# Six transposed rows instead of eight in block 1, two pair sums on GpSimd, and new call orders

## The chip, the cores and the metric

One core of one Trainium2 chip. The metric is the device time of one execution in microseconds. The kernel before takes 512.92 us, the median of three runs (512.43 to 513.56). TensorE multiplies matrices (PE in the profile; its weight loads are PEld), VectorE is DVE, ScalarE is ACT, GpSimd is POOL, and SyncE (SP) only issues DMAs.

## The reference

The input is 8 sequences of 1024 tokens with 128 features. Per token and head (16 heads of 8 columns) a state of 8 by 8 is decayed and added to, and read with the query; then come a layer norm, a gate, an output projection, a residual with its layer norm, and a feed-forward net of ternary weights with a second residual and norm.

```python
def step(state, inp):
    qt, kt, vt, gt = inp
    state = state * gt[..., None] + vt[..., None] * kt[..., None, :]
    out_t = jnp.einsum('bhij,bhj->bhi', state, qt)
    return (state, out_t)
...
out = (out - mu) * rsqrt(var + EPS) * gamma + beta
out = (out * silu(x @ Wg)) @ Wout
x = layernorm(x + out)
h = silu(tlin(x, w1_w, w1_s)) * tlin(x, w2_w, w2_s)
h = gelu(tlin(h, h1_w, h1_s))
h = gelu(tlin(h, h2_w, h2_s))
x = layernorm(x + tlin(h, w3_w, w3_s))
```

## The kernel before

**Blocks.** The 8192 tokens are cut into 16 blocks of 512; two blocks make a sequence. All products are float32. For each block n the attention half makes five projections of the transposed input (K, Q, F, V, gate; L2234), sends K and Q out to DRAM and fetches them back spread over the partitions as eight rows j of 512 tokens (KJ and QJ, 128 x 4096 each). VectorE and GpSimd multiply K by V (`kv`, `kv_gp`), VectorE runs one scan per row (`scan(n, j)`, L1582) and multiplies Q by the state, two rows at a time (`qs(n, p)`, L1589, p = 0 to 3).

**The sum of the eight rows.** For blocks 2 to 15, VectorE adds pairs down to one (`add(n, p)`, L1597, three calls), GpSimd adds the last two rows (`add_gp(n)`, L550), and TensorE transposes that single row, one 128 x 128 transpose for each of four chunks (`sum_transposed(n)`, L2293). Block 1 (`EARLY`, L27) leaves the adding to TensorE: for each chunk it transposes eight rows into the same PSUM accumulation, 32 transposes, and waits for all four `qs`. Block 0 has its own code (`kvj`, `qsj`, `sum_j`).

**Behind the sum.** `stats_o` (DVE), `rstd_of(n, "o")` (POOL), `norm_o` (ACT), `transpose_y` (PE), `affine` (ACT), `gated_y` (POOL), `attention_out` (PE), `residual_1` and `stats_1` (DVE), `rstd_of(n, "1")` (POOL), `norm_1` (ACT), `transpose_x1` (PE), `x1_hi` (ACT), `x1_lo` (DVE). Then the feed-forward half of the block: `up_hi`/`up_lo`, `mid_open`/`mid_hi`/`mid_lo` for two layers (all L2325) and `last_begin`/`last_rest` (L2424). Every activation is split into a high part on ACT (`hi`, L899) and a low part on POOL (`lo`, L482).

**What sets the order.** Each engine runs one list of calls, written out by hand in the file, from L562 (POOL), L989 (ACT), L1718 (DVE), L308 on (SP, the DMA queue) and L2465 on (PE). An engine works through its list strictly in order, and each call waits for semaphores. The attention half of block n+1 is interleaved with the feed-forward half of block n on all engines. The same queue order holds for DMAs: all transfers but one are issued by SP.

**The start.** Before the feed-forward lists, PE runs the attention of block 0 and part of block 1, with filler products that nobody reads (`keep_busy`, L2230; `keep_busy(16, F[3])` at L3171 is 16 of them). ACT copies the feed-forward weights to another format in four pieces (`split_weights(k)`, L967, L969) and sums the low halves of their bits (`sum_low_parts(k)`, L971, L980). DVE and PE make of these sums a flag (`find_low_parts`, `count_low_parts`, `set_flag`, L1716). PE waits for the flag behind `project_q(2)`, loads it (L3179) and branches to `rest(False)` or `rest(True)`: the feed-forward products, `up_hi(0, 0)` first, stand behind that branch. `center_w3` (L938, with L943 and L947) removes the mean of the last weight matrix on ACT, after `scale_w3` on POOL (L558); `last_begin(0)` needs it. `tanh(3)` (L828) reads the same PSUM bank that `project_gate(2)` writes next.

Of the kernel before, what the change touches and what calls it, by code (L numbers as in the profile page):

```python
# [3 lines left out]
def build_program(nc, x_d, xT_d, wproj_d, wffn_d, w3_d, w3s_d, cols_d, ident_d, out_d):  # L4
# [10 lines left out]
    P, T, HD = 128, 512, 8  # L15
# [11 lines left out]
    EARLY = range(1, 2)  # L27
    XB, XTB, GB = 4, 4, 3
# [9 lines left out]
    with ctx:  # L38
# [84 lines left out]
        def adds_gpsimd(n):  # L123
            return sum(m not in EARLY for m in range(1, n))

# [119 lines left out]
        def _(e):  # L245
            def load_x(n):
# [8 lines left out]
                4: (qj_made, 8), 5: (gate_made, 2), 6: (q_made, 2), 7: (v_made, 4), 8: (gate_made, 5), 9: (v_made, 6), 10: (gate_made, 7), 11: (gate_made, 8), 12: (gate_made, 9), 13: (gate_made, 10), 14: (gate_made, 11), 15: (v_made, 12),  # L255
# [73 lines left out]
            send(1, 1)  # L329
            load_weights(2)  # L330
            fetch(1, 1, 0)
            fetch(1, 1, 1)
# [3 lines left out]
            load_x(0)  # L336
            send(2, 1)
            load_xT(4)
            fetch(1, 0, 0)
            fetch(1, 0, 1)  # L340
            fetch(2, 1, 0)
            send(3, 1)
            send(2, 0)
            fetch(2, 1, 1)
            fetch(2, 0, 0)
            send(3, 0)
            load_x(1)
            fetch(2, 0, 1)
            fetch(3, 1, 0)
            fetch(3, 1, 1)  # L350
            load_x(2)
            send(4, 1)
            send(4, 0)
            load_xT(5)
            fetch(3, 0, 0)
            fetch(3, 0, 1)
            fetch(4, 1, 0)
            fetch(4, 1, 1)
            load_x(3)
            fetch(4, 0, 0)  # L360
            send(5, 0)
            load_x(4)
            send(5, 1)
            store(0)
            fetch(4, 0, 1)
            fetch(5, 1, 0)
            load_xT(6)
            load_x(5)
            fetch(5, 0, 0)
            load_xT(7)  # L370
            fetch(5, 0, 1)
            fetch(5, 1, 1)
            send(6, 1)
            fetch(6, 1, 0)
            load_x(6)
            send(6, 0)
            store(1)
            load_x(7)
            fetch(6, 1, 1)
            store(2)  # L380
            fetch(6, 0, 0)
            fetch(6, 0, 1)
            send(7, 1)
            fetch(7, 1, 0)
            load_xT(8)
            load_x(8)
            fetch(7, 1, 1)
            load_xT(9)
            send(7, 0)
            load_x(9)  # L390
            send(8, 1)
            fetch(7, 0, 0)
            fetch(7, 0, 1)
            fetch(8, 1, 0)
            send(8, 0)
            store(3)
            load_xT(10)
            send(9, 1)
            fetch(8, 0, 0)
            fetch(8, 1, 1)  # L400
            load_x(10)
            fetch(8, 0, 1)
            load_xT(11)
            store(4)
            load_xT(12)
            send(9, 0)
            fetch(9, 1, 0)
            fetch(9, 1, 1)
            fetch(9, 0, 0)
            fetch(9, 0, 1)  # L410
            send(10, 1)
            send(10, 0)
            fetch(10, 1, 0)
            fetch(10, 0, 0)
            send(11, 1)
            fetch(10, 1, 1)
            store(5)
            fetch(11, 1, 0)
            store(6)
            load_x(11)  # L420
            fetch(11, 1, 1)
            load_x(12)
            send(11, 0)
            load_xT(13)
            fetch(10, 0, 1)
            fetch(11, 0, 0)
            fetch(11, 0, 1)
            store(7)
            send(12, 1)
            send(12, 0)  # L430
            fetch(12, 1, 0)
            fetch(12, 1, 1)
            fetch(12, 0, 0)
            send(13, 0)
            send(13, 1)
            fetch(12, 0, 1)
            load_xT(14)
            fetch(13, 1, 0)
            fetch(13, 0, 0)
            store(8)  # L440
            fetch(13, 1, 1)
            load_x(13)
            send(14, 1)
            fetch(13, 0, 1)
            load_x(14)
            load_xT(15)
# [3 lines left out]
            load_x(15)  # L450
            store(9)
            fetch(14, 0, 0)
            fetch(14, 0, 1)
            send(15, 1)
            fetch(15, 1, 0)
            fetch(15, 1, 1)
            store(10)
# [18 lines left out]
        def _(e):  # L476
# [87 lines left out]
            scale_w3()  # L564
            qsj_gp(1)
            kvj_gp(2)
            kvj_gp(4)
            qsj_gp(2)
# [3 lines left out]
            kv_gp(1, 5)  # L572
            rstd_of(0, "o")
            kv_gp(1, 6)
# [5 lines left out]
            rstd_of(1, "o")  # L580
            kv_gp(2, 6)
            lo(1, 0, 3)
# [10 lines left out]
            rstd_of(2, "o")  # L593
            lo(1, 1, 2)
            lo(1, 1, 3)
            kv_gp(3, 6)
# [3 lines left out]
            kv_gp(3, 7)  # L600
            lo(2, 1, 1)
            rstd_of(2, "1")
            lo(2, 1, 2)
            lo(2, 1, 3)
            add_gp(3)
            lo(1, 2, 0)
            kv_gp(4, 6)
            rstd_of(3, "o")
            lo(1, 2, 1)
            lo(1, 2, 2)  # L610
            lo(1, 2, 3)
            kv_gp(4, 7)
# [3 lines left out]
            lo(2, 2, 2)  # L616
            rstd_of(3, "1")
            lo(2, 2, 3)
            add_gp(4)
            rstd_2(1)  # L620
            lo(1, 3, 0)
            lo(1, 3, 1)
            lo(1, 3, 2)
            rstd_of(4, "o")
            lo(1, 3, 3)
            rstd_2(2)
            kv_gp(5, 6)
# [2597 lines left out]
```

## Time and profile before

| | us |
|---|---|
| median of three runs | 512.92 |
| the profiled execution | 513.06 |
| its span | 511.3 |
| PE busy | 500.1 |
| DVE busy | 448.2 |
| ACT busy | 404.9 |
| POOL busy | 310.0 |

The profile lists the busy time of each engine and, for groups of instructions, how many there are, how long one takes and what ended the idle time before them. A busy PE is not a PE at its peak: its matmuls are pipelined, a record covers the time from issue to the last result, and the records of neighbours overlap, so that the pace is read from the start of one group to the start of the next. A product of 512 float32 columns appears as two records. The timeline gives the start of each group in microseconds from the start of the span, its length, and the idle time before it with the instruction that ended it.

### The profile page before, as it was taken

The numbers are of one execution on the slowest core, as the hardware profiler recorded it, in microseconds if no ns is written. First come the engines' busy times: TensorE is split into PE (matmuls) and PEld (weight loads), VectorE is DVE, ScalarE is ACT, GpSimd is POOL, SyncE is SP. The second block draws the span as 40 slices with busy tenths as digits, with TensorE's granted clock in tenths as the row PEclk, the third lists the DMA queues.
The fourth block names the chain that finished last, engine by engine and source line by source line (L and its number), as shares of the span: only waits on it lengthen the run. The fifth ranks groups of instructions, "written<-read, shape, count | busy, mean of one in ns | idle before, by whom it ended". The sixth has DMA issues, their size and how long they took to land.

```text
span 511.3 us, 7950 instructions
## 1 busy us (share of the span) xinstructions
PE 500.1 (98%) x2524; PEld 382.4 (75%) x2524; DVE 448.2 (88%) x707; ACT 404.9 (79%) x837; POOL 310.0 (61%) x363
## 2 busy tenths in 40 slices
PE   8999999999999999999999999999999999999995
PEld 4566777777878777787877877787777777787895
DVE  4799899999999999999999899999999999992352
ACT  4766778788897888889798887988787897878863
POOL 1651856848393856848385774828477674929431
PEclk9999999999999999999999999999999999999999
DMA  6988999809978666987988992389858870700001
GB/s 203 254 251 201 248 235 272 210 2 251 243 167 225 144 153 174 219 220 203 237 201 187 252 251 68 110 200 214 197 137 213 204 182 7 185 22 1 22 2 65
DMA packets 21500, 87.33 MB, mean 171 GB/s; under 512 B 2512, under 2 KB 3280, under 8 KB 13520
## 3 DMA queue, kind: packets, MB, share of 16 engines
q1 hardware_dynamic: 21312, 86.53, 68.1%
q8 instruction: 22, 0.36, 0.3%
q10 hardware_dynamic: 144, 0.26, 0.1%
q14 instruction: 22, 0.18, 0.1%
HBM read 74.72 MB, written 12.06 MB: 170 GB/s over the span
## 4 chain that ended last, share of the span: by engine, by line
PE 74%; POOL 10%; issue 8%; ACT 4%; DVE 3%; POOLq 0%; DVEq 0%; ACTq 0%
PE F L2325 43%; PE front L2234 8%; PE back L2424 8%; PE ps_v L2234 3%; POOL h2lo L482 3%; POOL h1lo L482 2%; PE back L2218 2%; PE back L2311 2%; PE back L2234 1%; PE F L2230 1%; ACT h L906 1%; PE back L2293 1%; POOL KJ L544 1%; DVE h L1646 1%; POOL QJ L550 1%
## 5 line engine op out<-in xcount | busy, mean ns | idle before, releaser
L482 POOL TENSOR_TENSOR h1lo<-h,h1hi 128x512 fp32r<-128x512 f32 x60 | 76.4, 1289 | 21.3 <-ACT h1hi L899 21.0
L906 ACT ACTIVATE h<-F,cols 128x512 f32<-128x512 f32 x120 | 79.9, 687 | 9.1 <-PE F L2325 8.1
L550 POOL TENSOR_TENSOR QJ<-QJ 128x512 f32<-128x512 f32 x14 | 17.9, 1281 | 110.3 <-DVE QJ L1597 110.3
L482 POOL TENSOR_TENSOR h2lo<-h,h2hi 128x512 fp32r<-128x512 f32 x60 | 76.3, 1291 | 5.0 <-ACT h2hi L899 4.5
L1582 DVE TENSOR_TENSOR_SCAN KJ<-g,carry,KJ 128x512 f32<-128x512 f32 x64 | 78.1, 1263 | 0.4 <-ACT carry L832 0.2
L2325 PE MATMUL F<-h2hi,whi 128*128 128x512 f32 (+1 forms) x256 | 76.7, 429 | 0.7 <-ACT h L906 0.4
L1582 DVE TENSOR_TENSOR_SCAN KJ<-g,KJ 128x512 f32<-128x512 f32 x64 | 74.3, 1203 | 2.6 <-POOL KJ L531 2.4
L2325 PE MATMUL F<-h1hi,whi 128*128 128x512 f32 (+1 forms) x256 | 71.4, 417 | 1.1 <-DVE h L1646 0.7
L1589 DVE TENSOR_TENSOR QJ<-QJ,KJ 128x1024 f32<-128x1024 f32 x60 | 71.5, 1218 | 0.2
L2325 PE MATMUL F<-h2lo,whi 128*128 128x512 f32 (+1 forms) x256 | 65.9, 399 | 0.0
L2325 PE MATMUL F<-h1lo,whi 128*128 128x512 f32 (+1 forms) x256 | 65.3, 397 | 0.0
L2234 PE MATMUL front<-xT,wproj 128*128 128x512 f32 x122 | 63.3, 601 | 0.8 <-ACT qk L822 0.6
L2325 PEld LDWEIGHTS F<-h2hi,whi 128*128 128x128 f32 x256 | 46.9, 189 | 22.2 <-issue 8.4
L2325 PEld LDWEIGHTS F<-h1hi,whi 128*128 128x128 f32 x256 | 45.6, 188 | 22.7 <-issue 9.5
L2424 PEld LDWEIGHTS back<-w,h 128*128 128x128 f32 x480 | 57.6, 192 | 2.6 <-DVE x1lo L1641 0.7
L2424 PE MATMUL back<-w,h 128*128 128x128 f32 x480 | 58.4, 275 | 0.0
L893 ACT ACTIVATE h<-F,cols 128x512 f32<-128x512 f32 x60 | 40.5, 686 | 17.5 <-PE F L2325 17.2
L2325 PEld LDWEIGHTS F<-h2lo,whi 128*128 128x128 f32 x256 | 45.7, 189 | 11.7 <-POOL h2lo L482 2.1
L2325 PEld LDWEIGHTS F<-h1lo,whi 128*128 128x128 f32 x256 | 46.2, 188 | 11.1 <-issue 1.4
L1566 DVE TENSOR_TENSOR KJ<-ps_v,KJ 128x1024 f32<-128x1024 f32 x44 | 52.7, 1209 | 1.4 <-ACT v_sb L867 1.4
L1597 DVE TENSOR_TENSOR QJ<-QJ 128x1024 f32<-128x1024 f32 x42 | 51.2, 1219 | 1.4
L1646 DVE SCALAR_TENSOR_TENSOR h<-F,cols,h 128x512 f32<-128x512 f32 x60 | 44.0, 744 | 6.1 <-ACT h L893 5.7
(176 smaller groups left out, 930.0 us busy)
## 6 DMA issues: line engine op xcount, KB each, us to landing
KJ<-qk_bounce SPq DMA_DIRECT2D x30, 1024.0 KB, 11.8
QJ<-qk_bounce SPq DMA_DIRECT2D x30, 1024.0 KB, 12.4
qk_bounce<-qk SPq DMA_DIRECT2D x30, 256.0 KB, 3.4
x_in<-in_x SPq DMA_DIRECT2D x16, 256.0 KB, 8.5
xT<-in_xT SPq DMA_DIRECT2D x15, 256.0 KB, 9.8
out<-res SPq DMA_DIRECT2D x15, 256.0 KB, 3.8
wraw<-in_wffn SPq DMA_DIRECT2D x2, 1024.0 KB, 10.3
wraw<-in_wffn SPq DMA_DIRECT2D x2, 256.0 KB, 4.5
```

Of the source, the lines that this page charges most:

```text
L482: e.tensor_tensor(h_lo[layer][:, t, :w], h[:, t, :w], h_hi[layer][:, t, :w].bitcast(f32), ALU.subtract).then_inc(lo_done[layer], 1)
L550: e.tensor_tensor(first, first, other, ALU.add).then_inc(add_gp_done, 1)
L893: e.activation(h[:, t, :WIDTH[n]], F[2 * (t % 2)][:, :WIDTH[n]], ACT.Silu, scale=S1[t]).then_inc(silu_done, 1)
L906: e.activation(dst[:, t, :WIDTH[n]], F[t][:, :WIDTH[n]], ACT.Gelu, scale=scale[t]).then_inc(gelu_done[layer], 1)
L1566: e.tensor_tensor(K, vb, K, ALU.mult).then_inc(kv_done, 1)
L1582: e.tensor_tensor_scan(K, g[:, :WIDTH[n]], K, init, ALU.mult, ALU.add).then_inc(scan_done, 1)
L1589: e.tensor_tensor(Q, Q, rows(KJ, n)[:, 2 * p:2 * p + 2, :], ALU.mult).then_inc(qs_done, 1)
L1597: e.tensor_tensor(first, first, other, ALU.add).then_inc(add_done, 1)
L1646: e.scalar_tensor_tensor(h[:, t, :w], F[2 * (t % 2) + 1][:, :w], S2[t], h[:, t, :w], ALU.mult, ALU.mult).then_inc(hmul_done, 1)
L2234: return e.matmul(bank[:, :WIDTH[n]], weights, xT[n % XTB][:, :WIDTH[n]], start=True, stop=True)
L2325: return e.matmul(out, whi[:, cs], part, start=start, stop=stop)
L2424: return e.matmul(back[:, chunk(c)], h3[:, k, chunk(c)], w3[:, k, :], start=k == 0, stop=k == NH - 1)
```

## The change

In block 1 GpSimd adds rows 0+1 and rows 2+3 (`add_pair(1, 0)`, `add_pair(1, 1)`) and TensorE transposes six rows per chunk (0, 2, 4, 5, 6, 7) instead of eight. `sum_transposed(1)` now waits also for the two adds. The counts of the semaphore that `add_gp` raises are shifted by two. Besides, the lists of all engines are in another order; the same calls stand in them, `add_pair` aside: 118 of the 146 calls of SP stand elsewhere in their list, and 209 of 468 on DVE, 343 of 545 on ACT, 342 of 731 on PE. `XT_READ[15]` waits for another projection.

```diff
     EARLY = range(1, 2)
+    EARLY_PAIRS = 2
...
         def adds_gpsimd(n):
-            return sum(m not in EARLY for m in range(1, n))
+            return sum(EARLY_PAIRS if m in EARLY else 1 for m in range(1, n))
...
+            def add_pair(n, p):
+                e.wait_ge(qs_done, NPAIR * (n - 1) + p + 1)
+                first, other = (rows(QJ, n)[:, k, :] for k in (2 * p, 2 * p + 1))
+                e.tensor_tensor(first, first, other, ALU.add).then_inc(add_gp_done, 1)
...
                 if n in EARLY:
                     e.wait_ge(qs_done, NPAIR * n)
-                else:
-                    e.wait_ge(add_gp_done, adds_gpsimd(n + 1))
-                terms = HD if n in EARLY else 1
+                e.wait_ge(add_gp_done, adds_gpsimd(n + 1))
+                terms = [*range(0, 2 * EARLY_PAIRS, 2), *range(2 * EARLY_PAIRS, HD)] if n in EARLY else [0]
```

SP, the start of its list:

```diff
             load_projections(0)
+            load_weights(0)
+            load_weights(1)
             load_constants()
             load_xT(1)
-            load_weights(0)
             load_projections(1)
-            load_weights(1)
-            load_w3()
+            load_weights(2)
+            send(1, 1)
```

POOL, the start (the list behind `lo(1, 0, 0)` changes as well):

```diff
             qsj_gp(0)
-            scale_w3()
+            kvj_gp(2)
             qsj_gp(1)
-            kvj_gp(2)
+            qsj_gp(2)
...
+            scale_w3()
             rstd_of(0, "1")
+            add_pair(1, 0)
+            add_pair(1, 1)
             lo(1, 0, 0)
```

ACT, the start:

```diff
-            split_weights(0)
+            split_weights(2)
+            sum_low_parts(0)
             silu_gate(0)
-            center_w3()
             copy_v(1)
             save_carry(0)
+            sum_low_parts(1)
             g_of_tanh(1)
             copy_q(1)
+            sum_low_parts(2)
             tanh(2)
             silu_gate(1)
             norm_o(0)
+            affine(0)
+            sum_low_parts(3)
             tanh(3)
-            affine(0)
-            split_weights(1)
-            sum_low_parts(3)
-            split_weights(2)
             silu_gate(2)
             split_weights(3)
+            copy_v(2)
             norm_1(0)
+            x1_hi(0)
             copy_k(3)
-            x1_hi(0)
+            copy_q(2)
...
             hi(1, 0, 2)
-            copy_k(4)
+            center_w3()
             hi(1, 0, 3)
```

DVE around the flag, and near the end:

```diff
             half_norm("1")
+            qs(1, 0)
+            scan(1, 7)
             set_flag()
-            qs(1, 0)
+            x1_lo(0)
             qs(1, 1)
-            x1_lo(0)
-            scan(1, 7)
             qs(1, 2)
...
             qs(15, 3)
             add(15, 1)
+            add(15, 2)
             hmul(14, 0)
-            add(15, 2)
```

PE keeps its list up to the branch. Behind it projections move between the products of the feed-forward net, and transposes by one or two calls; `project_gate(15)` goes from behind `up_lo(14, 3)` to block 13. The order within the last block changes too.

```diff
                 mid_open(2, 13, 1, low_parts)
+                project_gate(15)
                 mid_open(2, 13, 2, low_parts)
...
                 up_lo(14, 3, low_parts)
-                project_gate(15)
                 mid_open(1, 14, 0, low_parts)
```

## Rows read from the trace of the kernel before

**Rows 1.** The page: span, then busy time, share and instructions by engine.
```profile
span 511.3 us, 7950 instructions
PE 500.1 (98%) x2524; PEld 382.4 (75%) x2524; DVE 448.2 (88%) x707; ACT 404.9 (79%) x837; POOL 310.0 (61%) x363
```

**Rows 2.** Busy time by stretch: PE, PEld, DVE, ACT, POOL, granted clock, DMA share, GB/s.
```profile
92.20:455.00 362.80, 360.84 (x1764) 276.24 (x1763) 347.82 (x513) 302.85 (x626) 236.96 (x271) 1.00 0.72 177
455.00:480.00 25.00, 24.29 (x126) 18.99 (x125) 9.08 (x25) 20.21 (x45) 17.89 (x22) 1.00 0.03 11
480.00:501.50 21.50, 21.50 (x186) 21.50 (x185) 10.71 (x33) 15.22 (x39) 6.99 (x10) 1.00 0.04 14
```

**Rows 3.** Timeline: the sum of block 1 on PE.
```profile
52.04 3.66 PE L2293 MATMUL back<-ident,QJ 128*128 128x128 f32 x32
```

**Rows 4.** Timeline of GpSimd: its first `lo`, with the pause before it.
```profile
53.09 2.52 POOL L482 TENSOR_TENSOR h1lo<-h,h1hi 128x512 fp32r<-128x512 f32 x2 [10.15 <-ACT h1hi L899]
```

**Rows 5.** Instructions of one line: GpSimd's add; DVE's Q times state, 40-52 and 60-460.
```profile
L550 POOL TENSOR_TENSOR QJ<-QJ x14: 1271/1281/1297, 80.6 to 457.5; 128x512 f32<-128x512 f32 x14
...
L1589 DVE TENSOR_TENSOR QJ<-QJ,KJ x4: 1189/1203/1204, 44.1 to 50.6; 128x1024 f32<-128x1024 f32 x4
...
L1589 DVE TENSOR_TENSOR QJ<-QJ,KJ x56: 1195/1215/1368, 63.8 to 453.3; 128x1024 f32<-128x1024 f32 x56
```

**Rows 6.** Timeline of ScalarE, 31 to 45: tanh(2), affine(0), sum_low_parts(3).
```profile
31.36 0.69 ACT L828 ACTIVATE th<-front,half_bf 128x512 f32<-128x512 f32 x1 [2.43 <-PE front L2234]
35.83 0.78 ACT L873 ACTIVATE y<-back,cols 128x512 f32<-128x512 f32 x1
37.02 1.90 ACT L980 ACTIVATE h<-wraw 128x2048 f32<-128x2048 uint16 x1
```

**Rows 7.** Timeline of PE, 39 to 47: from project_gate(2) to the first up product.
```profile
39.05 1.02 PE L2234 MATMUL front<-xT,wproj 128*128 128x512 f32 x2
39.92 3.73 PE L2230 MATMUL F<-wproj,ident 128*128 128x128 f32 x32
45.66 1.12 PE L2234 MATMUL front<-xT,wproj 128*128 128x512 f32 x2
46.77 0.49 PE L2325 MATMUL F<-x1hi,whi 128*128 128x512 f32 x1
```

**Rows 8.** Timeline: x1hi on ScalarE; the flag and what follows it on DVE.
```profile
45.51 0.59 ACT L886 ACTIVATE x1hi<-back 128x512 fp32r<-128x512 f32 x1
44.02 0.14 DVE L1716 CAST flag<-F 1x1 int32<-1x1 f32 x1
44.09 2.34 DVE L1589 TENSOR_TENSOR QJ<-QJ,KJ 128x1024 f32<-128x1024 f32 x2
46.95 1.26 DVE L1582 TENSOR_TENSOR_SCAN KJ<-g,carry,KJ 128x512 f32<-128x512 f32 x1
...
50.58 1.20 DVE L1589 TENSOR_TENSOR QJ<-QJ,KJ 128x1024 f32<-128x1024 f32 x1
```

**Rows 9.** Timeline: hi(1, 0, 3) on ScalarE, and transpose_y(1) on PE.
```profile
57.09 0.62 ACT L899 ACTIVATE h1hi<-h 128x512 fp32r<-128x512 f32 x1
60.44 0.63 PE L2218 MATMUL back<-ident,o_norm 128*128 128x128 f32 x4 [0.16 <-ACT o_norm L851]
```

**Rows 10.** Instructions of two lines: the activations of center_w3 on ScalarE.
```profile
L943 ACT ACTIVATE x<-w x4: 293/296/301, 24.3 to 25.2; 128x128 f32<-128x128 f32 x4
...
L947 ACT ACTIVATE w<-w,w_mean x4: 386/387/402, 25.6 to 26.5; 128x128 f32<-128x128 f32 x4
```

**Rows 11.** Timeline, 455 to 461: the last add of block 15, its sum, its gate.
```profile
455.58 0.75 DVE L1646 SCALAR_TENSOR_TENSOR h<-F,cols,h 128x512 f32<-128x512 f32 x1
456.25 1.22 DVE L1597 TENSOR_TENSOR QJ<-QJ 128x1024 f32<-128x1024 f32 x1
457.54 1.28 POOL L550 TENSOR_TENSOR QJ<-QJ 128x512 f32<-128x512 f32 x1 [9.32 <-DVE QJ L1597]
458.88 0.66 PE L2293 MATMUL back<-ident,QJ 128*128 128x128 f32 x4 [0.33 <-POOL QJ L550]
```

More of the change, by code:

```diff
@@ L1069, in _ @@
             hi(1, 1, 3)
+            tanh(4)
             norm_o(2)
+            square(0)
             affine(2)
@@ L1073, in _ @@
             hi(2, 1, 0)
-            tanh(4)
             gelu(1, 1, 1)
@@ L1152, in _ @@
             gelu(2, 3, 2)
+            copy_v(6)
             gelu(2, 3, 3)
+            norm_2(2)
             silu(4, 0)
-            tanh(7)
-            g_of_tanh(6)
-            copy_v(6)
             silu(4, 1)
@@ L1199, in _ @@
             hi(1, 5, 3)
-            norm_2(3)
+            copy_k(8)
             affine(6)
@@ L1205, in _ @@
             hi(2, 5, 1)
-            copy_q(8)
-            gelu(1, 5, 2)
-            hi(2, 5, 2)
-            gelu(1, 5, 3)
-            tanh(8)
-            copy_v(8)
-            square(4)
-            hi(2, 5, 3)
-            norm_1(6)
-            gelu(2, 5, 0)
-            g_of_tanh(8)
-            gelu(2, 5, 1)
-            x1_hi(6)
-            copy_k(9)
-            gelu(2, 5, 2)
-            gelu(2, 5, 3)
+            gelu(1, 5, 2)
+            gelu(1, 5, 3)
+            hi(2, 5, 2)
+            hi(2, 5, 3)
+            square(4)
+            copy_q(8)
+            gelu(2, 5, 0)
+            norm_1(6)
+            gelu(2, 5, 1)
+            gelu(2, 5, 2)
+            x1_hi(6)
+            gelu(2, 5, 3)
+            copy_v(8)
+            tanh(8)
+            g_of_tanh(8)
             silu(6, 0)
+            save_carry(7)
             silu(6, 1)
@@ L1225, in _ @@
             hi(1, 6, 1)
+            copy_k(9)
             silu(6, 2)
@@ L1255, in _ @@
             silu(7, 0)
+            copy_k(10)
+            g_of_tanh(9)
+            silu(7, 1)
             hi(1, 7, 0)
-            silu(7, 1)
             silu(7, 2)
+            save_carry(8)
             hi(1, 7, 1)
@@ L1277, in _ @@
             hi(2, 7, 3)
-            norm_2(5)
+            tanh(10)
+            norm_2(6)
             norm_1(8)
-            copy_k(11)
-            g_of_tanh(10)
+            x1_hi(8)
             gelu(2, 7, 0)
             save_carry(9)
-            copy_v(10)
-            x1_hi(8)
             gelu(2, 7, 1)
@@ L1289, in _ @@
             silu(8, 0)
+            copy_v(10)
+            copy_k(11)
             silu(8, 1)
-            norm_2(6)
+            g_of_tanh(10)
             hi(1, 8, 0)
@@ L1343, in _ @@
             hi(2, 9, 2)
+            hi(2, 9, 3)
+            copy_q(13)
+            norm_1(10)
+            copy_k(13)
+            copy_v(12)
+            x1_hi(10)
+            gelu(2, 9, 0)
             norm_2(8)
-            hi(2, 9, 3)
-            norm_1(10)
-            gelu(2, 9, 0)
-            copy_q(13)
             gelu(2, 9, 1)
-            x1_hi(10)
-            g_of_tanh(12)
-            copy_v(12)
             gelu(2, 9, 2)
@@ L1867, in _ @@
             qs(5, 1)
+            add(5, 0)
+            x1_lo(4)
             qs(5, 2)
-            x1_lo(4)
-            add(5, 0)
             qs(5, 3)
@@ L1975, in _ @@
             qs(9, 1)
-            add(9, 0)
-            x1_lo(8)
             qs(9, 2)
             qs(9, 3)
+            x1_lo(8)
+            add(9, 0)
             add(9, 1)
@@ L2029, in _ @@
             qs(11, 1)
+            x1_lo(10)
+            add(11, 0)
             qs(11, 2)
             qs(11, 3)
-            x1_lo(10)
-            add(11, 0)
             add(11, 1)
+            add(11, 2)
             hmul(10, 0)
-            add(11, 2)
             hmul(10, 1)
@@ L2087, in _ @@
             qs(13, 3)
+            add(13, 0)
             add(13, 1)
@@ L2110, in _ @@
             qs(14, 1)
+            x1_lo(13)
+            add(14, 0)
             qs(14, 2)
-            add(14, 0)
-            x1_lo(13)
             qs(14, 3)
@@ L2948, in rest @@
                 mid_hi(2, 11, 3, low_parts)
-                project_k(15)
                 mid_lo(2, 11, 0, low_parts)
+                mid_lo(2, 11, 1, low_parts)
+                project_q(14)
                 transpose_x1(12)
-                mid_lo(2, 11, 1, low_parts)
                 mid_lo(2, 11, 2, low_parts)
+                up_hi(12, 0, low_parts)
                 mid_lo(2, 11, 3, low_parts)
-                up_hi(12, 0, low_parts)
+                up_lo(12, 0, low_parts)
                 last_begin(11)
-                up_lo(12, 0, low_parts)
                 up_hi(12, 1, low_parts)
@@ L2961, in rest @@
                 up_hi(12, 2, low_parts)
+                up_hi(12, 3, low_parts)
+                sum_transposed(13)
                 up_lo(12, 2, low_parts)
-                sum_transposed(13)
-                up_hi(12, 3, low_parts)
+                project_k(15)
                 up_lo(12, 3, low_parts)
```

924 lines of the change are left out of this document (457 added, 467 removed).

## The prediction

> **What bounds the kernel now.** I read the page first for the busy times, then the busy times by stretch, then the timelines of the start, of block 1 and of block 15. On the page PE is busy for 98% of the span and DVE for 88% [rows 1]. By stretch it is plainer [rows 2]: from 92.2 to 455.0 PE is busy for 360.8 of 362.8 us and DVE for 347.8 of 362.8, which is 96%, with hardly more between its instructions than their own spacing. Both engines are nearly full, ACT and POOL are not. From 455 on DVE has run out of scans (9.1 us busy of 25) and PE alone carries the rest: 24.3 of 25.0 and 21.5 of 21.5. So the end is set by PE's work, by when PE can begin it (the start), and by the few places where PE must wait for the chain of the attention half. A saving on PE counts in full only if no wait takes its place. The profiled execution took 513.06 us with a span of 511.3; what lies around the span is 1.8. My sum is made against 513.06, which is 0.14 above the median of 512.92.
>
> **Eight transposes less.** The 32 transposes of block 1 run from 52.04 with 3.66 us [rows 3]; with about 0.27 for the last record alone, the pace is (3.66 - 0.27)/31 = 0.11 us. Eight of them are 0.87 us. They stand on PE's list in the middle of work, between `up_lo(0, 3)` and `project_k(4)`, so this is a true saving of PE's work: **-0.9**.
>
> **Two adds on GpSimd.** `add_gp` takes 1.28 us [rows 5], and an `add_pair` has the same shape, so two cost 2.6 us. GpSimd sits idle for 10.15 us before its first `lo` [rows 4]: from 42.9 to 53.1, the row's start less its pause. The adds need `qs(1, 0)` and `qs(1, 1)`. In the new list of DVE `qs(1, 1)` comes behind `scan(1, 7)`, `set_flag` and `x1_lo(0)`; counted on from 44.1 in the durations of [rows 5, 8] it ends near 48.6, and the second add near 50, well before the sum at about 52 to 53. What is queued behind them is `lo(1, 0, 0)`, which isn't ready before 53. So the adds are free: **0**. If that cover were gone, it would be up to 2.6 on the sum. DVE works on while GpSimd adds: its `qs` takes 1.203 us with GpSimd idle and 1.215 in the median of the 56 that run beside a GpSimd that works on `lo` and `kv` [rows 5], so I price the neighbourhood at nothing; the longest of these 56, 1.368, is the upper bound, 0.2 for each.
>
> The Trainium skill says otherwise (SBUF — State Buffer, Who interferes with whom): a VectorE instruction with two SBUF inputs contends with a GpSimd instruction that reads SBUF, as an exclusive lock. By that rule each add would push a `qs` by up to its own 1.28 us, 2.6 in all. The medians of these rows differ by 0.01 us, so the trace doesn't bear this price out, and the sum goes without it.
>
> **The start.** PE's list is unchanged up to the branch, but ACT and DVE reach what it waits for later.
> - ACT has `sum_low_parts(2)` ahead of `tanh(2)` now. It is one of the two long ones, 1.90 us and a short read, near 2.0, as `sum_low_parts(3)` has at 37.02, while `tanh(2)` began at 31.36 after 2.43 us idle [rows 6]. With the other pieces put in front (`split_weights(2)`, `sum_low_parts(0)` and `(1)`), I count `tanh(2)` at 32.1: +0.75 up to `affine(0)`. DVE was busy with scans until it took up `gated_y0`, so most of this is hidden there.
> - `sum_low_parts(3)` now stands ahead of `tanh(3)`: `affine(0)`, which ran from 35.83 for 0.78 [rows 6], ends at 37.3, the sum takes 2.0, `tanh(3)` 0.7, so it ends at 40.0. `project_gate(2)` writes the bank that `tanh(3)` reads, and began at 39.05 [rows 7]. It moves by **+1.0**. Behind it PE has the 3.73 us of filler, `project_k(3)` and `transpose_x1(0)`, nothing of which shrinks.
> - `copy_k(3)` comes behind `x1_hi(0)` on ACT (0.59 us [rows 8]) and `project_q(2)` waits for it: **+0.6**. `set_flag` comes behind `qs(1, 0)` and `scan(1, 7)`, 1.2 + 1.26 us, at 46.8 instead of 44.02 [rows 8]. From `project_q(2)` to the first up product it was 1.1 us [rows 7], the load of the flag and the branch among it, and PE takes the flag up only behind `project_q(2)`, now at 47.3: the late flag is hidden by 0.5.
> The first up product thus starts at about 48.4 instead of 46.77: **+1.6**.
>
> **How much of this block 0 absorbs.** Between 46.77 and `transpose_y(1)` at 60.44 [rows 7, 9] lie 13.7 us with 12.6 of PE work in them (16 up and 16 mid products at 0.23, two projections at 0.86, the 3.5 of the sum). The other 1.05 are waits for `hmul` and ACT. If they vanish, all but 0.6 of the start's loss is absorbed; if they stay, nothing is. `copy_v(2)` has been done already, which takes 0.6 us from ACT in that stretch, but `center_w3` moves in ahead of `hi(1, 0, 3)`: it ran from 24.3 to 26.9, 2.6 us [rows 10]. `hi(1, 0, 3)` was at 57.09 and goes to about 59.2, when `mid_hi(1, 0, 3)` needs it (`transpose_y(1)`, right behind it, came at 60.44 [rows 9]): just hidden. I take **-0.6**, in the middle of 0 and -1.05.
>
> **Blocks 2 to 14.** Here the new lists change nothing in the work, only in the waits. PE waited some 2 us in 362.8 by its own row and DVE 15 [rows 2], part of it in small gaps. What can be gained is bounded by that; what can be lost isn't. I measured the PE work between `sum_transposed(n)`, `transpose_y(n)`, `attention_out(n)`, `transpose_x1(n)` and `up_hi(n, 0)` in both lists with the paces above: the shortest distance from the sum to `transpose_y` is 4.56 us in both, from there to `attention_out` 2.55 before and 2.78 after, to `transpose_x1` 5.9 before and 5.7 after. Only from `transpose_x1` to `up_hi` does the least distance fall, from 1.85 to 0.93 in blocks 9 and 12, and `x1_hi` alone takes 0.59 [rows 8]. That may cost a few tenths, other places gain as much: **0**, with -2 to +2 as bounds.
>
> **Block 15.** `add(15, 2)` started at 456.25 behind `hmul(14, 0)` (0.75) and PE then waited for GpSimd's add until 458.88, 0.33 us at least [rows 11]. In the new list the add comes ahead of that `hmul`, and `project_gate(15)` is already done, 0.86 us less work behind the sum; the same amount now stands before it. The gain is the wait: **-0.4**. The new order within the last block serves PE, which is full anyway [rows 2]: 0. The loads moved forward on SP (`load_weights(0)` to `(2)` ahead) delay the constants by 0.5 MB, about 1.5 us, and nothing needed them before 6.9: 0.
>
> **Sum.** -0.9 + 1.6 - 0.6 - 0.4 = -0.3 against 513.06: 512.8, or 512.6 against the median. I predict 512.6.
>
> **Rivals.**
> - *The saving and the block-15 gain come through, the start is absorbed.* If all 1.05 of waits in block 0 vanish and the middle gains 1 to 2 us from fewer waits, the time is 510.2 to 511.8. For it: PE's waits in block 0 are there in rows. Against it: ACT is the late one there and gets `center_w3` on top. Chance 0.36.
> - *The start's delay decides (slower).* If the flag or `tanh(3)` is later than I count (a weight piece that lands late holds ACT at `split_weights(2)`, say), the first up product starts beyond 49.5, and since DVE and PE are both full behind it nothing takes the loss back: from a delay of about 3 us on it outweighs 0.9 + 0.4 + 0.6, and the time is 514 to 515.5. For it: PE is 98% busy, so a late start is carried to the end. Chance 0.15.
> - *The middle has new waits (slower).* A transpose that comes too early holds PE, 0.3 us in each of six or more blocks: 514 to 515. Chance 0.11.
> - *The edit does nothing*, because the sum of block 1 waits for `qs(1, 3)` anyway and the eight transposes are replaced by a wait: 513.5. In the trace `qs(1, 3)` ended at 51.8 [rows 8] and the sum began at 52.04, so they were close; with a late start PE comes later than `qs`. Inside the forecast.
>
> **How the numbers follow.** Forecast and the do-nothing case together 0.38: 511.9 to 513.9. About 0.2% is what a measurement of this kernel can tell from no change, so faster means under 511.9. The chances are faster 0.36, same 0.38, slower 0.26. For 8 in 10 the range cuts a tenth at either side: 510.4 to 515.0; the likeliest case's own range is 511.9 to 513.9.
>
> **What would show it.** `sum_transposed(1)` should have 24 records and take 2.8 us; GpSimd should show two adds between 45 and 50 and no wait for them on PE; `project_gate(2)` should start near 40 and the first up product near 48.4; `transpose_y(1)` near 61; the add of block 15 should no longer hold PE. The prediction is wrong if the first up product is at 47 or at 50, or if the steady stretch is shorter or longer by over 2 us.

## The result and the profile after

The changed kernel takes 525.33 us, the median of 5 runs (525.19 to 526.13), against 513.44 for the kernel before (5 runs, 512.43 to 513.77): a ratio of 1.0236 with a 95% interval of 1.0225 to 1.0248, 11.9 us slower. The forecast was 512.6, with 515.0 as its upper end.

The page of the changed kernel, span and busy times, and then its busy time in the steady stretch (PE, PEld, DVE, ACT, POOL, granted clock, DMA share, GB/s):

```profile
span 523.5 us, 7936 instructions
PE 503.0 (96%) x2516; PEld 381.3 (73%) x2516; DVE 449.4 (86%) x707; ACT 403.4 (77%) x837; POOL 321.3 (61%) x365
...
92.20:455.00 362.80, 353.47 (x1712) 267.74 (x1711) 337.09 (x497) 291.10 (x602) 239.31 (x265) 1.00 0.70 175
```

PE, full in this stretch before with 360.84 us [rows 2], has lost 7.4 us of it, and DVE 10.7. The granted clock is 1.00 for both kernels as the mean of this long stretch; one short fall is hidden in it, and comes below. Over the whole span the engine that is busy for much longer is POOL, 321.3 instead of 310.0 us [rows 1] (PE has 2.9 more, DVE 1.2). Its two new adds are 3.5 of these 11.3, and another 7.3 are five operations that take longer than they did. The waits of the changed kernel show where (engine and line, what it waited for: us in total, times, longest), and below them is the row of GpSimd's `shift`, the last 128x4 operation of the layer norm behind the first residual (minimum/median/maximum in ns):

```profile
ACT x L859 <- POOL shift L517: 30.1, 13, 5.5
PEld back L2226 <- ACT x L859: 11.7, 10, 2.8
PE back L2226 <- ACT x L859: 7.3, 5, 2.1
...
L517 POOL TENSOR_TENSOR shift<-shift,rstd x16: 198/202/2449, 42.9 to 483.8; 128x4 f32<-128x4 f32 x16
```

The same two, of the kernel before; no row of PE waiting for `x` is among its waits:

```profile
ACT x L851 <- POOL shift L516: 18.7, 11, 2.9
...
L516 POOL TENSOR_TENSOR shift<-shift,rstd x16: 199/202/205, 42.7 to 472.8; 128x4 f32<-128x4 f32 x16
```

An operation of 0.20 us takes up to 2.45. What runs beside it is in the timeline of the changed kernel in block 4 (start, duration, engine, line, tiles, count, and in brackets the pause before it and what ended it):

```profile
157.69 1.00 POOL L515 TENSOR_TENSOR rstd<-rstd,mhalf 128x4 f32<-128x4 f32 x1
158.51 2.33 DVE L1597 TENSOR_TENSOR QJ<-QJ,KJ 128x1024 f32<-128x1024 f32 x2
158.77 2.13 POOL L517 TENSOR_TENSOR shift<-shift,rstd 128x4 f32<-128x4 f32 x1
161.00 1.65 ACT L859 ACTIVATE x<-x_in,shift,rstd 128x128 f32<-128x128 f32 x4 [5.48 <-POOL shift L517]
162.70 0.66 PE L2226 MATMUL back<-ident,x 128*128 128x128 f32 x4 [2.10 <-ACT x L859]
```

And the same place of the kernel before:

```profile
157.68 0.20 POOL L516 TENSOR_TENSOR shift<-shift,rstd 128x4 f32<-128x4 f32 x1
157.98 1.65 ACT L851 ACTIVATE x<-x_in,shift,rstd 128x128 f32<-128x128 f32 x4 [2.51 <-POOL shift L516]
158.04 3.47 DVE L1589 TENSOR_TENSOR QJ<-QJ,KJ 128x1024 f32<-128x1024 f32 x3
159.69 0.66 PE L2218 MATMUL back<-ident,x 128*128 128x128 f32 x4
```

Before, `shift` had ended 0.16 us ahead of VectorE's products. After, it begins 0.26 us behind the start of the first of them and ends at 160.90, with the second. `norm_1` and `transpose_x1` follow, and TensorE stands for 2.10 us. This happens in five blocks. The table has them from the timelines: start of `shift`, start of the product that it stands next to, length of `shift`, and the wait of TensorE before `transpose_x1`.

| block | before: shift, product | after: shift, product | shift takes | PE waits |
|---|---|---|---|---|
| 4 | 157.68, 158.04 | 158.77, 158.51 | 2.13 | 2.10 |
| 6 | 213.56, 214.15 | 218.89, 218.94 | 2.45 | 2.00 |
| 7 | 244.00, 245.50 | 252.55, 252.57 | 1.28 | 0.80 |
| 9 | 301.98, 304.72 | 312.82, 312.86 | 1.30 | 1.18 |
| 11 | 362.43, 363.88 | 373.29, 373.18 | 1.15 | 1.24 |

The five waits are 7.3 us, PE's whole row above. In ten of the other eleven blocks `shift` ends before a product begins, or VectorE has none there, and takes 0.20 us. In block 5 it begins at 190.02, the product at 190.17, and it takes 0.20 us as well.

One of the waits costs more than its length. Behind the 2.00 us of block 6 TensorE's granted clock falls to 0.50 (1.2 of 2.4 GHz), from 223.5 to 227.0. The row of that wait, and the busy times in the middle of this stretch:

```profile
223.14 0.83 PE L2226 MATMUL back<-ident,x 128*128 128x128 f32 x4 [2.00 <-ACT x L859]
...
223.50:226.50 3.00, 3.00 (x10) 2.09 (x8) 1.76 (x3) 1.99 (x5) 0.00 (x0) 0.50 0.48 131
```

The two records of a projection span 1.73 us there (225.48) instead of 1.02. Half the clock for 3.4 us is 1.7 us of TensorE's work, my estimate. Together with the five waits this makes 9.0 of the 11.9 us. The kernel before has its clock at 1.00 up to 505 us, and so has e9 below, which lacks the wait; a test of the clock by itself wasn't made.

Two things in the new lists make `shift` late against VectorE. In blocks 6, 7, 9 and 11, `rstd_of(n, "1")`, which `shift` ends, now stands behind `lo(2, n-1, 3)` instead of ahead of it, 1.3 us of GpSimd; in block 6 `rstd_2(4)` stands ahead of it too, and in block 9 `kv_gp(10, 7)`, 1.3 us each. In block 4 its place is unchanged, but ScalarE has `affine(4)` and `tanh(6)` ahead of its first `gelu(1, 3, 0)` now, and GpSimd starts its `lo` of that layer at 152.39 instead of 151.27.

### The profile page after: what moved, and what is told of

It is laid out like the page before. It is cut to its first block, busy times and chain, and to the rows that moved or that the text cites. A ratio compares the mean times of both kernels' runs of the same rounds, so it can differ in the third digit from the quotient of the medians.

```text
span 523.5 us, 7936 instructions
## 1 busy us (share of the span) xinstructions
PE 503.0 (96%) x2516; PEld 381.3 (73%) x2516; DVE 449.4 (86%) x707; ACT 403.4 (77%) x837; POOL 321.3 (61%) x365
## 4 chain that ended last, share of the span: by engine, by line
PE 41%; POOL 15%; issue 8%; ACT 7%; DVE 2%; POOLq 0%; DVEq 0%; ACTq 0%
PE F L2332 25%; PE back L2431 7%; POOL h2lo L483 5%; PE front L2242 3%; PE back L2226 2%; POOL shift L517 2%; POOL h1lo L483 2%; ACT x L859 1%; POOL KJ L545 1%; ACT h L914 1%; POOL rstd L515 1%; POOL rstd_o L515 1%; ACT h2hi L907 1%; PE back L2318 1%; POOL y L562 1%
## 5 line engine op out<-in xcount | busy, mean ns | idle before, releaser
L2332 PE MATMUL F<-h2hi,whi 128*128 128x512 f32 (+1 forms) x256 | 73.1, 419 | 0.1
L2332 PE MATMUL F<-h2lo,whi 128*128 128x512 f32 (+1 forms) x256 | 68.6, 407 | 0.1
L545 POOL TENSOR_TENSOR KJ<-KJ,v_sb 128x512 f32<-128x512 f32 x32 | 41.0, 1288 | 19.0 <-ACT v_sb L875 19.0
## 6 DMA issues: line engine op xcount, KB each, us to landing
QJ<-qk_bounce SPq DMA_DIRECT2D x30, 1024.0 KB, 11.9
```

What stands on the lines that cost most here:

```text
L545: e.tensor_tensor(K, K, v_sb[:, :WIDTH[n]], ALU.mult).then_inc(kv_gp_done, 1)
L2332: return e.matmul(out, whi[:, cs], part, start=start, stop=stop)
```

## The experiments

The first question was which half of the change costs the time: the pair sums or the orders. **e1** is the kernel before with the pair sums:

```diff
+            add_pair(1, 0)
+            add_pair(1, 1)
             lo(1, 0, 0)
...
-                terms = HD if n in EARLY else 1
+                terms = [*range(0, 2 * EARLY_PAIRS, 2), *range(2 * EARLY_PAIRS, HD)] if n in EARLY else [0]
```

> The kernel before with the two adds on GpSimd and 24 transposes instead of 32 in block 1, all lists in the order of before. Theory A (the change's loss comes from the new orders alone): the pairs save PE up to 0.9 us and cost nothing, so 0.0 to 0.9 us under the kernel before. Rival B (the pairs themselves do harm, by holding VectorE or by coming late): slower than before by 1 us or more, with PE waiting for the adds before its sum of block 1.

Measured: 514.13 us (12 runs, 513.12 to 514.84) against 513.76 (17 runs), ratio 1.0010 (1.0001 to 1.0019). No saving, rather 0.4 us lost. The eight transposes are gone, but what lies behind the sum doesn't come earlier. PE's timeline of e1:

```profile
53.84 2.78 PE L2300 MATMUL back<-ident,QJ 128*128 128x128 f32 x24
57.06 1.12 PE L2242 MATMUL front<-xT,wproj 128*128 128x512 f32 x2 [0.44 <-ACT qk L830]
57.62 4.29 PE L2332 MATMUL F<-h1hi,whi 128*128 128x512 f32 x16
62.21 0.63 PE L2226 MATMUL back<-ident,o_norm 128*128 128x128 f32 x4 [0.29 <-ACT o_norm L859]
```

From the start of the sum to `transpose_y(1)` it is 8.37 us, and before it was 60.44 - 52.04 = 8.40 [rows 3, 9]. PE comes 0.88 earlier to `project_k(4)`, whose bank ScalarE hasn't read yet, and waits. (The whole stretch lies later here by over a microsecond. The start moves by about that much from one execution to the next: the first `shift`, at 42.74 before and 42.93 after, was at 43.98 in e1 and at 44.2 in e2 and e3.)

**e2** is the changed kernel without the pair sums, with eight rows on TensorE:

```diff
-    EARLY_PAIRS = 2
+    EARLY_PAIRS = 0
...
-            add_pair(1, 0)
-            add_pair(1, 1)
```

> The changed kernel with the new lists, but eight rows transposed in block 1 and no add on GpSimd. Theory A (orders alone): about as slow as the changed kernel, 11 to 13 us above before, perhaps 0.9 more than the changed kernel. Rival B (the pairs): near the kernel before, within 2 us.

Measured: 524.99 us (4 runs, 523.09 to 527.49), ratio 1.0207 (1.0186 to 1.0227). The orders alone cost the time. TensorE's row of waits for `x` is again 7.3 us in five places, and the longest `shift` has 2448 ns.

**e3** puts the three small operations of the norm and the `pow` ahead of the last `lo` in eight blocks of the changed kernel. In seven of them they had moved; in block 4 they stood behind it before as well:

```diff
-            lo(2, 6, 3)
             rstd_of(7, "1")
+            lo(2, 6, 3)
```

> The changed kernel, but on GpSimd rstd_of(n, "1") stands ahead of lo(2, n-1, 3) again wherever it had moved behind it (n = 3, 4, 5, 6, 7, 9, 11, 12). Theory C: the loss is that the small multiply `shift` on GpSimd (0.2 us alone) starts while VectorE is in its Q-times-state products, waits until they end (1.15 to 2.45 us in five blocks), and holds norm_1 and transpose_x1. Then the five long shifts vanish or become fewer and the time falls by 5 to 10 us from the changed kernel. Rival D: the norm is late because the statistics or the queue of ScalarE are late, not because of this row; then the shifts go back to 0.2 us, but PE waits as before and the time changes by less than 2 us.

Measured: 523.10 us (4 runs, 522.09 to 523.55), ratio 1.0175 (1.0158 to 1.0193). All `shift`s are short again, and only 2.2 us came back, where 5 to 10 had been expected. The wait moved, since the last `lo` is now 1.6 us later and TensorE needs it as well. From the waits of e3 and its timeline in block 9:

```profile
PE F L2332 <- POOL h2lo L483: 5.8, 8, 2.0
...
311.84 0.50 PE L2332 MATMUL F<-h2lo,whi 128*128 128x512 f32 x1 [2.01 <-POOL h2lo L483]
```

So this run takes the long `shift` away and adds another delay. It could be read either way: the long `shift` as the cause, or as the sign of a GpSimd that is late anyway. Later runs decide that.

**e4** measures the collision by itself. In the kernel before, GpSimd idles for up to 9.3 us in each block while VectorE multiplies and adds; ten tiny operations go there, reads of two small tiles in odd blocks and `memset`s in even ones (one 128x128 add in blocks 13 and 14):

```diff
+            def probe(n):
+                e.wait_ge(qs_done, NPAIR * (n - 1) + 1)
...
+                    elif n % 2:
+                        e.tensor_tensor(probed[:, a:a + 4], eps4[:], minus4[:], ALU.add)
+                    else:
+                        e.memset(probed[:, a:a + 4], 0.0)
```

> The kernel before with small extra instructions on GpSimd ahead of add_gp(n), released when the first Q-times-state product of the block is done: for n = 3, 5, 7, 9, 11 ten adds of 128x4 that read constants in SBUF, for n = 4, 6, 8, 10, 12 ten memsets of 128x4, for 13 and 14 one add of 128x128. Theory C (GpSimd instructions that read SBUF wait for VectorE instructions with two inputs in SBUF): some of the small adds last 1 to 2.5 us instead of 0.2 and end together with a Q product or an add of VectorE, while all memsets stay near 0.1. Rival E (anything on GpSimd is held, or the slow shifts come from somewhere else): the memsets are as slow as the adds, or none is slow.

Measured: the reads take 0.20 us alone and up to 3.51, the `memset`s 0.10 all of the time. (The one run with these additions took 515.65 us.) The rows of both lines in e4, the reads in block 7 and VectorE beside them:

```profile
L562 POOL TENSOR_TENSOR probed<-eps,minus x50: 192/203/3508, 102.1 to 341.9; 128x4 f32<-128x4 f32 x50
L564 POOL MEMSET probed<- x50: 96/101/103, 130.1 to 366.5; 128x4 f32 x50
...
217.41 7.71 POOL L562 TENSOR_TENSOR probed<-eps,minus 128x4 f32<-128x4 f32 x9
...
217.39 2.34 DVE L1615 TENSOR_TENSOR QJ<-QJ,KJ 128x1024 f32<-128x1024 f32 x2
219.65 1.22 DVE L1623 TENSOR_TENSOR QJ<-QJ 128x1024 f32<-128x1024 f32 x1
220.78 0.69 DVE L1667 TENSOR_TENSOR x1lo<-back,x1hi 128x512 fp32r<-128x512 f32 x1
```

The first read began at 217.41, took 3.51 us and ended at 220.92, just past the end of the third of three VectorE instructions without a pause between them (219.65 + 1.22 = 220.87). Further reads took 1.18 beside a product or an add, and 0.20 beside `x1_lo`, `hmul` and `kv`. Beside scans it was the norm's own small reads that took 0.20 (at 156.30 and 156.45 in the kernel before, during the scans of 155.70 to 158.12). All of these have an input in PSUM. VectorE's products and adds, with both inputs in SBUF, are the only ones that were seen to hold GpSimd up. The `memset`s are a thinner test than their number says: the ten of a block take 0.39 us together. In block 6 all ten ran beside products (from 188.54, products from 187.27 to 190.75); in blocks 4, 8 and 12 the product began among them, and in block 10 they ran beside `x1_lo`.

The Trainium skill says just this (SBUF — State Buffer, Who interferes with whom): a VectorE instruction with two SBUF inputs contends with a GpSimd instruction that reads SBUF, not with one that only writes it. This case's runs agree, for the one with 3.51 us instead of 0.20 and for the other with 0.10 for the ten `memset`s of block 6.

Three more runs tried to move parts of the change. **e5** gives `shift` to VectorE, so that no GpSimd operation has to pass at that point:

```diff
             scan(5, 7)
+            shift_v(4)
...
-            rstd_of(4, "1")
+            rstd_v(4)
```

> The changed kernel, but for blocks 2 to 15 the multiply `shift` of the first norm is done by VectorE (one small instruction behind the last scan of the next block, ahead of the Q products that held it) instead of GpSimd. Lists otherwise as changed. Theory C (the port is the main price): the waits of transpose_x1, 8.1 us in five places, shrink to under 2 us in all, and the time falls to 516 to 519. Rival F (GpSimd's chain is late anyway, since the new lists give it the same work later against VectorE and PE; the port only shows it): PE's waits go elsewhere and the time stays above 521.

Measured: 528.88 us (4 runs, 527.7 to 529.9), ratio 1.0302 (1.0286 to 1.0318), slower than the changed kernel by 3.5. The operation is short on VectorE, but it stands behind `scan(n+1, 7)` in a full list. e5 in block 10:

```profile
338.00 3.61 DVE L1601 TENSOR_TENSOR_SCAN KJ<-g,carry,KJ 128x512 f32<-128x512 f32 x3
341.53 0.14 DVE L1637 SCALAR_TENSOR_TENSOR shift<-mv,rstd 128x4 f32<-128x4 f32 x1
...
343.46 0.66 PE L2262 MATMUL back<-ident,x 128*128 128x128 f32 x4 [2.54 <-ACT x L870]
...
PE back L2262 <- ACT x L870: 10.1, 7, 3.1
```

In the changed kernel GpSimd had this `shift` at 340.97, some 4 us before VectorE's next product, and PE didn't wait for it. Here it waits 2.54. The last row is TensorE's of the whole run: the waits of over 0.9 us are in blocks 2, 3, 8, 10, 13 and 14, and none of them is in the five blocks. So the long `shift`s are gone and new waits, 10.1 us, have come where there was none. The expected 516 to 519 was wrong.

**e7** is the changed kernel with VectorE's whole list of before, **e8** with SyncE's. (The diffs are those of the change, reversed for one engine.)

> The changed kernel with VectorE's whole list as before (the other four as changed). If the collisions come from VectorE's new order (scans ahead of residual_1 and stats_1, products earlier), the long shifts vanish and the time falls by 3 us or more. If they come from the other lists, it stays within 2 us of the changed kernel.

> The changed kernel with the DMA queue's list as before. My reading is that no transfer holds an engine in either kernel: within 1 us of the changed kernel. Rival: late fetches push VectorE, and the time falls by 2 us or more.

Measured: e7 544.42 us (4 runs, 543.47 to 544.91), ratio 1.0601 (1.0585 to 1.0617); e8 559.98 us (4 runs, 558.78 to 563.08), ratio 1.0921 (1.0894 to 1.0948). One row of each:

```profile
PEld F L2332 <- DVE h L1654: 17.0, 21, 2.4
...
POOL KJ L545 <- DMA KJ<-qk_bounce: 32.9, 3, 18.7
```

In e7 the feed-forward half waits for `hmul`; in e8 GpSimd waits for a fetch for up to 18.7 us, on a queue that works strictly in order. In e8, 17 of the 46 us (estimated as above) are TensorE's clock, which is at 0.50 in several stretches. Neither was expected: e7 was to be 3 us or more faster than the changed kernel or within 2 us of it, e8 within 1 us of it or 2 us faster. Both runs say that the lists fit only each other. They tell nothing of which list of the changed kernel costs the 11.9 us, and exchanging one list was the wrong instrument for that.

**e6** is the kernel before with the edits at block 15 alone:

```diff
+            add(15, 2)
             hmul(14, 0)
-            add(15, 2)
...
+                project_gate(15)
```

> The kernel before with two edits alone: add(15, 2) ahead of hmul(14, 0) on VectorE, and project_gate(15) in block 13 on PE. By the step of the prediction: 0.4 us faster than before (0 to 0.9). Rival: the gate product ahead of the sum of block 15 only moves PE's work, no change.

Measured: 514.19 us (11 runs) against 513.77 (15 runs), ratio 1.0006 (0.9997 to 1.0015). The gain of 0.4 isn't there. PE's wait has changed its cause: before, it was for GpSimd's add [rows 11]; in e6 it is for `hmul`, which now stands behind the add:

```profile
459.84 0.60 PE L2293 MATMUL back<-ident,QJ 128*128 128x128 f32 x4
...
460.83 0.73 PE L2325 MATMUL F<-x1hi,whi 128*128 128x512 f32 x2 [0.39 <-DVE h L1646]
...
463.60 2.60 PE L2325 MATMUL F<-h1hi,whi 128*128 128x512 f32 x10 [1.10 <-DVE h L1646]
```

The last row is a second wait for `hmul`. Before, it was 0.24 us (at 462.03), and `project_gate(15)` stood just ahead of it, at 460.30. This product filled the wait; taken away, with its 0.86 us, it leaves 0.86 us more of waiting.

**e9, e10 and e11** take up what e3 left open. e9 is the changed kernel in which VectorE waits, at the five places, until `shift` is over:

```diff
+    BEHIND_SHIFT = ((5, 0), (7, 0), (8, 1), (10, 0), (12, 1))
...
             def qs(n, p):
+                if (n, p) in BEHIND_SHIFT:
+                    e.wait_ge(shift_done["1"], n)
```

> The changed kernel, in which VectorE's first product Q times state behind scan(n+1, 7) waits for GpSimd's shift of the norm of block n, for n = 4, 6, 7, 9 and 11, the five places at which that 128x4 operation took 2.13, 2.45, 1.28, 1.30 and 1.15 us beside VectorE's products instead of 0.20. Nothing else is changed: neither the order of any engine nor the time at which GpSimd comes to the shift. Theory L (the long shifts are what the change costs): each of the five ends within 0.25 us of its start again, VectorE begins its product 0.3 to 0.6 us later, the waits of TensorE before transpose_x1 at 160, 221, 255, 315 and 375 us (8.1 us together) shrink to 0 to 0.5 each, and the time falls from 525.3 to 517 to 520. Theory G (GpSimd and ScalarE are late anyway, the long shift only shows it, as e3_rstd_early could be read): another wait takes their place and the time stays at 522 to 525.

Measured: 516.85 us (4 runs, 516.65 to 517.27) against 514.00 (7 runs), ratio 1.0060 (1.0043 to 1.0077). Five waits added to the engine that is second fullest take 8.5 us off the time, a little more than the expected 517 to 520 allowed. Counted against the kernel before of each series, 11.9 and 2.85 us, it is 9.0, about as much as the five waits and the lost clock together. So the rival reading of e3, a GpSimd that is late anyway, explains at most what is left. The clock stays at 1.00 between 92 and 455 us in e9. e9, the row of `shift`, its wait row for ScalarE's `x`, and block 4:

```profile
L518 POOL TENSOR_TENSOR shift<-shift,rstd x16: 198/201/203, 43.3 to 475.6; 128x4 f32<-128x4 f32 x16
PEld back L2229 <- ACT x L860: 4.4, 10, 0.7
...
159.19 0.20 POOL L518 TENSOR_TENSOR shift<-shift,rstd 128x4 f32<-128x4 f32 x1
159.43 2.36 DVE L1600 TENSOR_TENSOR QJ<-QJ,KJ 128x1024 f32<-128x1024 f32 x2 [0.41 <-POOL shift L518]
161.19 0.66 PE L2229 MATMUL back<-ident,x 128*128 128x128 f32 x4 [0.16 <-ACT x L860]
```

VectorE paid 0.41 us, and TensorE's wait fell from 2.10 to 0.16.

e10 brings the collision into the kernel before: in the same five blocks `shift` is held until `scan(n+1, 7)` is done, and in the last four `rstd_of` stands behind `lo(2, n-1, 3)`. e11 is e10 with the wait of e9 on top, so that `shift` is just as late but alone:

```diff
+                if k == "1" and n in LATE:
+                    e.wait_ge(scan_done, HD * (n + 2))
                 e.tensor_tensor(sh, sh, r, ALU.mult).then_inc(shift_done[k], 1)
...
+                if (n, p) in BEHIND_SHIFT:
+                    e.wait_ge(shift_done["1"], n)
```

(The lines above "..." are in both, the lines below in e11 alone.)

> The kernel before, in which GpSimd's shift of the norm of block n waits for scan(n+1, 7) on VectorE, for n = 4, 6, 7, 9 and 11, so that it comes to run beside the products that follow that scan; in the last four the three small operations of the norm stand behind lo(2, n-1, 3) instead of ahead of it, so that the wait holds nothing of the layer. Theory L: the shifts take 1.2 us (n = 9, one product) to 3.5 us (n = 6 and 7, two products and an add), some 10 to 13 us together where five alone take 1.0; TensorE waits before the transposes of these blocks and the time is 519 to 525. Theory G (a late shift is taken up by slack): 514 to 516.

> e10_late_shift and nothing else but that VectorE's first product behind scan(n+1, 7) waits for that shift, in the five blocks: the shift is as late as in e10, but no product runs beside it. Theory L: the shifts take 0.20 us each, VectorE loses 0.3 us in each of the five, TensorE waits only for the lateness itself, and the time is 3 us or more under that of e10, at 514.5 to 518. Theory G: e10 and e11 differ by less than 1 us. Rival O (the later place of the three operations is the cost and not their length): both are above 518.

Measured: e10 532.46 us (4 runs, 529.06 to 536.86), ratio 1.0358 (1.0286 to 1.0431); e11 523.06 us (4 runs, 522.72 to 523.52), ratio 1.0181 (1.0163 to 1.0199). Running beside the products costs 9.4 us and the lateness alone, with VectorE's waits for it, another 9.1. Both are more than expected: e10 lies above its 519 to 525 and e11 above its 514.5 to 518, where the rival of the later place had put it. So in this pair lateness and length share the cost about evenly. Here `shift` waits for the last scan, and is later against TensorE than in the changed kernel, where e9 leaves 2.85 us for lateness and all else.

The 9.4 us aren't all waiting. TensorE's waits for `x`, of e10 and of e11, and its clock in e10:

```profile
PE back L2221 <- ACT x L854: 13.3, 5, 4.5
...
PE back L2224 <- ACT x L855: 7.0, 5, 2.6
...
224.00:230.50 6.50, 5.96 (x18) 4.99 (x19) 3.73 (x4) 5.18 (x10) 0.00 (x0) 0.50 0.37 112
```

The waits differ by 6.3 us. In e10 the clock is at 0.50 behind three of them (4.53, 2.17 and 3.47 us), for 17 us in all, and in e11 behind one (2.65 us), for 3.4: 8.5 and 1.7 us of work, by the same estimate. The four times of e10 go with this: 529.06, 531.01, 533.9 and 536.86 us at mean granted clocks of 0.995, 0.988, 0.983 and 0.981.

The longest `shift` of e10 took 1.03 us, not the expected 1.2 to 3.5: the operations ahead of it were held instead. In block 6 of e10 three of the four operations of the norm came beside the products, each held by one product or add:

```profile
218.14 2.33 DVE L1592 TENSOR_TENSOR QJ<-QJ,KJ 128x1024 f32<-128x1024 f32 x2
218.16 1.23 POOL L512 TENSOR_TENSOR rstd<-mv,eps 128x4 f32<-128x4 f32 x1
219.34 1.19 POOL L513 TENSOR_TENSOR shift<-mv,minus 128x4 f32<-128x4 f32 x1
220.39 1.21 DVE L1600 TENSOR_TENSOR QJ<-QJ 128x1024 f32<-128x1024 f32 x1
220.49 1.99 POOL L515 TENSOR_TENSOR rstd<-rstd,mhalf 128x4 f32<-128x4 f32 x1
```

What remains open: e9 is still 2.85 us above the kernel before. Its largest wait on PE is the second one of e6, 1.00 us at 464.53 (0.99 at 472.79 in the changed kernel), and comes with the moved `project_gate(15)`. Putting this product back alone wasn't tried; the others are small and spread. None of the kernels beats the one before.

## Why the prediction was wrong

**Eight transposes less, -0.9.** The size is right: 24 records, 2.84 us instead of 3.66 [rows 3].

```profile
52.86 2.84 PE L2300 MATMUL back<-ident,QJ 128*128 128x128 f32 x24
...
60.46 0.63 PE L2226 MATMUL back<-ident,o_norm 128*128 128x128 f32 x4 [0.18 <-ACT o_norm L859]
```

"A true saving of PE's work" holds only together with the new orders: from the sum's start to `transpose_y(1)` it is 7.60 us here and 8.37 in e1. By itself the saving ends in a wait for ScalarE, 0.44 us at `project_k(4)`, and e1 gained nothing.

**Two adds on GpSimd, 0.** Timeline of GpSimd, changed kernel:

```profile
45.51 1.27 POOL L556 TENSOR_TENSOR QJ<-QJ 128x512 f32<-128x512 f32 x1 [2.38 <-DVE QJ L1597]
48.47 2.21 POOL L556 TENSOR_TENSOR QJ<-QJ 128x512 f32<-128x512 f32 x1 [1.70 <-DVE QJ L1597]
```

They lie in the pause, end at 50.68 and hold nobody, as forecast. But the second takes 2.21 instead of 1.27, held by the product beside it. The step that failed is the one by which I set the rule of the Trainium skill aside. I compared the four products of 40 to 52 with "the 56 that run beside a GpSimd that works" [rows 5]. They don't: GpSimd waits for exactly these products (`add_gp` had paused for 9.32 us [rows 11]), so both medians, 1.203 and 1.215, are mostly of VectorE with GpSimd idle and can't tell the rule right or wrong. The one row that could, the longest of 1.368, I took as a bound. It is a trace of the collision: at 274.97 that product began while a `lo` of 273.95 to 275.26 was still reading. And I priced only VectorE's side. The other side, a small GpSimd operation held by a chain of VectorE's, is the dear one.

**The start, +1.6, and what block 0 absorbs, -0.6.** `project_gate(2)` came at 39.31 (counted: near 40), the first up product at 48.05 (48.4), which is +1.3. The sum began 0.8 later than before, so about 0.5 was absorbed, and with the shorter sum `transpose_y(1)` is at 60.46 against 60.44. The forecast was "near 61". As a single execution moves by a microsecond here, this is as near as it can be.

**Blocks 2 to 14, 0 with -2 to +2.** This is the term that was wrong, and the step behind it is the one named above, the neighbourhood of GpSimd and VectorE priced at nothing. Some 11 of the 11.9 us are lost here: `transpose_y(1)` is at 60.46 and was at 60.44, while the last `shift` is at 483.8 and was at 472.8. I counted the distances on TensorE's list alone, the least work between `transpose_x1` and its neighbours, and found one that shrinks, by 0.9 us in blocks 9 and 12. The waits are in blocks 4, 6, 7, 9 and 11, and come from elsewhere. What differs is where GpSimd's `rstd_of(n, "1")` stands against VectorE's products, on two lists that I hadn't laid beside each other. The rival "a transpose that comes too early holds PE, 0.3 us in each of six or more blocks" had the place and the sign, but not the cause or the size: the transpose wasn't early, its input was late, and it was five blocks and 0.8 to 2.1 us each. e9 shows that 8.5 us hang on these five operations being held; 1.7 of them are the slower clock behind one of the waits, for which the prediction had no term at all.

**Block 15, -0.4.** Not there (e6). Where PE waits for the later of two, taking the add first only puts `hmul` second. And `project_gate(15)`, counted as "0.86 us less work behind the sum", had been filling a wait for `hmul`: 0.24 us with it, 1.10 without it in e6.

**The sum** missed by 12.7 us. (A slip beside it: by its own terms the faster rival reaches from 510.2 to 511.2, not to 511.8.) Its bounds were those of waits seen before. Nothing in the trace of before showed a long `shift`, and that was no evidence: it missed the products by 0.16 us in block 4 and by 0.39 in block 6.

## What to carry to other kernels

When call orders change on an engine that shares with another, list for both engines which short operations lie near which long ones, with the margin in time. A margin of 0.2 us in the trace of before is a cost of 2 us waiting. Ask of two medians whether both conditions really occur in them before you dismiss a rule with them. And where a short operation of GpSimd feeds the critical chain, let VectorE wait those few tenths: a wait of 0.4 us on the fuller engine bought 2 us on the fullest. Look at the granted clock in short stretches behind each wait, too: a mean of 1.00 over 360 us hid a fall that cost 1.7.

## What was unexpected of the hardware

- A GpSimd read isn't let in between two VectorE instructions for sure. The `shift` of block 4 took 2.13 us across two products and the read of e4 3.51 across three instructions, while three operations of e10's block 6 were each held by one instruction only, and most of e4's later reads, 1.18 us each, as well. What decides between the two wasn't found.
- The recorded start doesn't tell who was first. In block 6 `shift` is recorded at 218.89, 0.05 us ahead of the product at 218.94, and still took 2.45 us. In block 5 it is 0.15 us ahead, still running when the product is recorded to begin, and took 0.20.
- It works both ways. In e1 the product at 49.39 took 1.77 us instead of 1.20, since an `add_pair` was reading until 50.07:

```profile
46.61 3.46 POOL L556 TENSOR_TENSOR QJ<-QJ 128x512 f32<-128x512 f32 x2 [2.43 <-DVE QJ L1597]
49.39 1.77 DVE L1597 TENSOR_TENSOR QJ<-QJ,KJ 128x1024 f32<-128x1024 f32 x1
```

- TensorE's clock can fall behind a wait of 2 us. It did in the changed kernel and in e2 behind the same wait (2.00 and 1.98 us in block 6), and not in e9, which doesn't have this wait. But it didn't fall behind the 2.10 us of block 4, nor behind the 2.54 and 3.07 of e5's profiled run. What decides wasn't found.
